# Two layers of a transformer-like block on one core: first layer and second attention in one engine block, last stores waited for by name

## What is computed

```python
x = x + tanh(g_xattn[0]) * L0_xattn(layernorm(x), ctx, ...)   # 16 heads, soft triangular mask
x = x + tanh(g_ffn[0])   * L0_ffn(layernorm(x), ...)          # 8 experts, best 2 per row, capacity per expert
x = x + tanh(g_xattn[1]) * L1_xattn(layernorm(x), ctx, ...)   # rotary positions, causal band of 128
x = x + tanh(g_ffn[1])   * L1_ffn(layernorm(x), ...)          # 16 experts, best 4 per row, and 2 shared ones
```

## Time and profile before

| what | us |
| --- | --- |
| median of 3 runs | 1760.22 |
| profiled execution, its own time | 1755.15 |
| its span, first to last instruction | 1753.3 |
| TensorE busy in it | 1574.9 (90%) |
| VectorE busy | 1237.1 (71%) |
| ScalarE busy | 1001.0 (57%) |
| GpSimd busy | 774.6 (44%) |

### The profile page before, as it was taken

The page is one execution under the profiler, slowest core; times in us unless marked ns, Lnnn a source line. Parts: engine busy times, 40 slices in busy tenths (PEclk is TensorE's granted clock), DMA queues, the critical chain, the costliest instruction groups (busy, mean ns, idle before and its releaser), DMA issues. The chain is left out here.

```text
span 1753.3 us, 45015 instructions
## 1 busy us (share of the span) xinstructions
PE 1574.9 (90%) x16664; PEld 1223.8 (70%) x16664; DVE 1237.1 (71%) x3676; ACT 1001.0 (57%) x1742; POOL 774.6 (44%) x948
## 2 busy tenths in 40 slices
PE   4799999789899999999999578898887689999997
PEld 3466666458788888888887345665554389898874
DVE  5888888856556555655577489988987366757767
ACT  5578877665345454445433355675654358677752
POOL 4356657787310000100264433332465153677765
PEclk8999999989999999999999689999999799999999
DMA  6555545243376535545462343332334456899954
GB/s 197 131 144 120 118 110 136 52 116 99 96 193 197 192 118 181 187 138 189 134 184 82 87 85 86 65 69 54 74 85 128 157 166 216 259 299 295 313 167 144
DMA packets 297740, 257.03 MB, mean 147 GB/s; under 512 B 198079, under 2 KB 270187, under 8 KB 296248
## 3 DMA queue, kind: packets, MB, share of 16 engines
q1 hardware_dynamic: 271288, 168.84, 35.7%
q0 software_dynamic: 26240, 85.32, 14.8%
HBM read 102.98 MB, written 107.74 MB: 120 GB/s over the span
## 5 line engine op out<-in xcount | busy, mean ns | idle before, releaser
L1830 PE MATMUL ps<-m_xT,m_w_halves 128*128 128x256 f16 x3360 | 413.4, 273 | 0.0
L1830 PEld LDWEIGHTS ps<-m_xT,m_w_halves 128*128 128x128 f16 x3360 | 329.1, 98 | 38.8 <-ACT a_probs L1283 0.4
L1283 ACT ACTIVATE a_probs<-ps 128x1024 f32<-128x1024 f32 (+1 forms) x256 | 234.6, 917 | 161.7 <-PE ps L1108 158.3
L1861 PE MATMUL ps<-m_w_halves,m_hiddenT 128*128 128x256 f16 x1680 | 231.2, 274 | 8.8 <-DVE m_hiddenT L1989 5.8
L1915 ACT ACTIVATE m_hiddenT<-m_hidden 128x256 f16<-128x256 f32 x280 | 116.4, 416 | 213.1 <-DVE m_hidden L1984 213.1
L1409 POOL TENSOR_TENSOR a_probs<-a_probs,a_half_above 128x512 f32<-128x512 f32 x128 | 163.8, 1282 | 127.7 <-ACT a_probs L1283 127.2
L1989 DVE TENSOR_TENSOR m_hiddenT<-m_hidden,m_hiddenT 128x256 f16<-128x256 f32 x280 | 119.1, 425 | 124.5 <-ACT m_hiddenT L1915 124.2
L1108 PE MATMUL ps<-a_Q,a_K 32*128 32x256 f16 (+1 forms) x2048 | 146.5, 262 | 65.4 <-DVE a_neg_max L1498 30.0
L1781 POOL DMA_DIRECT2D expert_out<-m_y x40 | 29.0, 725 | 382.0 <-DVE m_y L1972 189.6
L1501 DVE TENSOR_REDUCE a_qT<-ps 128x4 f16<-128x1024 f32 x128 | 156.6, 1223 | 44.4 <-PE ps L1119 43.6
L1861 PEld LDWEIGHTS ps<-m_w_halves,m_hiddenT 128*128 128x128 f16 x1680 | 163.7, 98 | 33.0 <-DVE m_hiddenT L1989 10.9
(11 more groups left out here) (312 smaller groups left out, 3015.3 us busy)
## 6 DMA issues: line engine op xcount, KB each, us to landing
routed<-m_zeros POOLq DMA_DIRECT2D x32, 768.0 KB, 4.2
r_space<-routed SPq DMA_DIRECT2D x48, 512.0 KB
routed_out<-m_y SPq DMA_DIRECT2D x48, 512.0 KB
r_w_load<-in_L_w SPq DMA_DIRECT2D x24, 896.0 KB, 7.1
dispatched<-r_x_halves SPq DMA_DIRECT2D x10, 1024.0 KB, 5.2
expert_out<-m_y POOLq DMA_DIRECT2D x40, 256.0 KB, 2.6
a_ctx_in<-in_ctx SPq DMA_DIRECT2D x32, 256.0 KB, 2.9
m_experts_load<-in_L_experts SPq DMA_DIRECT2D x18, 384.0 KB, 3.5
```

Of the source, the lines that this page charges most:

```text
L1283: A(pr[:, g % 2, 2 * jp:2 * jp + 2, :], SC[:, :, 0:SPAN], ACT.Exp, scale=1.0 / math.sqrt(DH)).then_inc(asem["ex"], 1)
L1830: last = mm(psum[:, v % HB, m * CH:(m + 1) * CH], wh[u][:, ws_, m, d_ * F0 + f_ * P:d_ * F0 + (f_ + 1) * P], xT[:, q % XB, xs_ * KT + d_, ...
L1861: last = mm(down_of(q, t), hT[:, hs_, f_, t * P:(t + 1) * P], wh[u][:, ws_, 2, f_ * D:(f_ + 1) * D], start=f_ == 0 and k == 0, stop=f_ == ...
```

## The change

The bodies of the five lists of `attention` become functions that `attention` returns (they stand one step of indentation further left and are otherwise as they were, but for the lines below). After both calls one block runs, on each engine, the first layer's list and the second attention's behind it. In place of the meeting between them SyncE, TensorE, ScalarE and GpSimd wait at the start of their second list for `m0f_y_out` at 40 (the last take), for the stores of the second layer's weights and for the zeroing; VectorE waits for the latter two only. The waits for the stores of `m_y` stand ahead of ScalarE's first exponential and of GpSimd's first gather of the second attention. The waits at the end of the first layer's lists go. In `last_rows` the take stands behind the statistics. The meeting ahead of the second layer's experts stays.

```diff
-        with nc.Block() as block:
 
-            @block.sync
-            def _(sp):
+        def sync(sp):
+            if causal_band:
+                first_layer_ended(sp)
...
-            @block.tensor
-            def _(pe):
+        def tensor(pe):
+            if causal_band:
+                first_layer_ended(pe)
...
-            @block.scalar
-            def _(act):
+        def scalar(act):
+            if causal_band:
+                first_layer_ended(act)
             A = nc.scalar.activation
 
             def exp(i, s):
                 g, jp = step(s)
                 need(act, "sc", i, s)
+                if causal_band and (i, s) == (0, 0):
+                    all_rows_stored(act)
...
-            @block.gpsimd
-            def _(pool):
+        def gpsimd(pool):
+            if causal_band:
+                first_layer_ended(pool)
...
                     newton(i, s)
+                    if causal_band and (i, s) == (min(GATHER_AT), 0):
+                        all_rows_stored(pool)
                     if causal_band and i in GATHER_AT:
...
-            @block.vector
-            def _(dve):
+        def vector(dve):
+            if causal_band:
+                first_layer_sent(dve)
...
+        return sync, tensor, scalar, gpsimd, vector
...
+    rows_stored = [sem(f"m0f_y_sent{u}") for u in range(2)]
+
+    rows_out = sem("m0f_y_out")
+    w16_sent = [sem(f"m0f_experts1_sent{u}") for u in range(2)]
+    routed_zeroed = sem("m0f_zeroed")
+    ROUTED_ZEROED = 16 * RG * (ROUTED // (P * 6))
+
+    def first_layer_sent(eng):
+        for u in range(2):
+            eng.wait_ge(w16_sent[u], 16 * 9)
+        eng.wait_ge(routed_zeroed, ROUTED_ZEROED)
+
+    def first_layer_ended(eng):
+        eng.wait_ge(rows_out, CHUNKS0)
+        first_layer_sent(eng)
+
+    def all_rows_stored(eng):
+        for u in range(2):
+            eng.wait_ge(rows_stored[u], 16 * (CHUNKS0 // 2))
...
                 store_next_layer(E1 - 1)
-                for u in range(2):
-                    sp.wait_ge(e_sent[u], 16 * (E1 // 2))
...
-                for u in range(YB):
-                    pool.wait_ge(y_sent[u], 16 * (STEPS // YB))
-                pool.wait_ge(zeroed, 16 * RG * PIECES)
...
             def last_rows(dve):
-                take(dve, STEPS - 1)
                 row_stats(dve, 1, 10)
                 mean_and_var(dve, 1, 10)
+                take(dve, STEPS - 1)
...
-    attention(0)
+    first_layer = attention(0)
     open_route1()
-    attention(1)
+    second_layer = attention(1)
+
+    with nc.Block() as block:
+
+        @block.sync
+        def _(sp):
+            first_layer[0](sp)
+            second_layer[0](sp)
...
```

More of the change, by code:

```diff
@@ new lines, in sync, with load, to_slots, slots_of_k @@
+        def sync(sp):
+            if causal_band:
+                first_layer_ended(sp)
+            def load(m):
+                need(sp, "tc", m - 2)
+                sp.dma_start(xin[:, m % 2, :, :], ctx_dram[m, :, :, :]).then_inc(ctx_in[m % 2], 16)
+            def to_slots(m, src, dst, counter):
+                need(sp, "sc", m - 4, 7)
+                need(sp, "max", m - 4, 7)
+                for t in range(TT):
+                    sp.dma_start_transpose(dst[:, m % 4, :, t * P:(t + 1) * P],
+                                           src[:, t, :, :].rearrange("p h r -> p (h r)"))\
+                      .then_inc(slots_in[counter][m % 4], 16)
+            def slots_of_k(m):
+                need(sp, "kh", m)
+                to_slots(m, kT1, K1, "k1")
+                need(sp, "kl", m)
+                to_slots(m, kT2, K2, "k2")
+            def half_of_q2(m, k):
+                if causal_band:
+                    need(sp, "neg", m, k)
+                else:
+                    need(sp, "max", m, 4 * k + 3)
+                need(sp, "qdup", m)
+                need(sp, "sc", m - 1, 4 * k + 3)
+                for t in range(TT):
+                    sp.dma_start_transpose(Q2[:, 2 * k:2 * k + 2, t * P:(t + 1) * P],
+                                           qT2[:, m % 3, t, k * 8:(k + 1) * 8, :].rearrange("p h r -> p (h r)"))\
+                      .then_inc(q2_in[k], 16)
+            load(0)
+            load(1)
+            if causal_band:
+                for k, name in (("L1_router", "router"), ("L1_e_bias", "e_bias"), ("iota", "iota"), ("less", "less"),
+                                ("tri", "tri")):
+                    whole = r1[name][:, :] if name in ("e_bias", "iota") else r1[name][:, :, :]
+                    sp.dma_start(whole, a[k]).then_inc(ld1, 16)
+                sp.wait_ge(buffers_set, 3)
+            for i in range(-3, B):
+                if 0 <= i:
+                    half_of_q2(i, 1)
+                if causal_band and 0 <= i + 2 < B:
+                    slots_of_k(i + 2)
+                if 2 <= i + 5 < B:
+                    load(i + 5)
+                if 0 <= i + 1 < B:
+                    half_of_q2(i + 1, 0)
+                if not causal_band and i == -2:
+                    sp.dma_start(x[:, 8 * TT:16 * TT, :], x_dram[:, 8 * TT:16 * TT, :]).then_inc(x_loaded[2], 16)
+                if not causal_band and 0 <= i < 10:
+                    if i == 0:
+                        sp.wait_ge(zero_set, 1)
+                    sp.dma_start(disp[i * P * 8:(i + 1) * P * 8, :].rearrange("(p t) d -> p (t d)", p=P),
+                                 r_xhl[:, 2, :, :, :].rearrange("p t s d -> p (t s d)").bitcast(F32))\
+                      .then_inc(disp_zeroed, 16)
+                if not causal_band and i == 10:
+                    for m, k in enumerate(("w1", "w3", "w2")):
+                        sp.dma_start(w_load[:, m, :], a[f"L0_{k}"][0, :, :]).then_inc(w_loaded, 16)
+                if i + 3 < B:
+                    need(sp, "qh", i + 3)
+                    need(sp, "ql", i + 3)
+                    to_slots(i + 3, qT1, Q1, "q1")
+                    if not causal_band:
+                        slots_of_k(i + 3)
+            if not causal_band:
+                first.sync(sp)
+            if causal_band:
+                sp.wait_ge(combined, 4 * B)
+                sp.dma_start(shared_weights(), w16[:, :, E1:E1 + 2, :]).then_inc(w1_in[0], 16)
+                sp.wait_ge(sent1[0], RT * 4 * 16)
+                for r in range(XB1):
+                    load_routed_rows(sp, r)
```

1163 lines of the change are left out of this document (557 added, 606 removed).

## The result

The changed kernel took 1749.36 us in the median of 4 runs (1748.31 to 1752.44), the kernel before 1759.47 in 4 runs beside them (1756.6 to 1761.05). The ratio is 0.9947, 95% interval 0.993 to 0.9964: 9.3 us less, between 6.3 and 12.3. Two later sets of runs of the same kernel gave 0.9947 (0.9928 to 0.9967) and 0.9961 (0.9947 to 0.9976). The forecast was 7.4 us less, a ratio of 0.9958, which all three intervals hold.

The account below looks back on a forecast made before the run. Bound by the meeting between layers, no engine, half its hole GpSimd's DRAIN. -8.21 + 0.25 + 0.2 + 0.4 + 0 = -7.36 us against the 1760.22 median gives 1752.9 us (chance 0.70), range 1749.5 to 1756.2.

Parts of the forecast that it names:

- The meeting, -8.21: Between first layer's last take and second attention: removing the meeting saves the whole 8.21 us hole, at least 5.3.
- the waits, +0.2: Second attention's start: seeing the take's count and passing three fulfilled waits costs 0.2 us, bounds 0.05 and 0.6.
- The take behind the statistics, +0.25: End of first layer on VectorE: statistics fill an idle gap, last copy ends 0.25 us later, bounds 0 and 1.02.
- Context load beside the store, +0.4: Second attention's opening: first context load shares transfer engines with GpSimd's last store, costing 0.4 us, bounds 0 and 0.73.
- GpSimd's memsets, 0: Second attention's opening: memsets move 6.7 us earlier, the rest 7.4; GpSimd's 4.5 us idle covers the difference, so 0.
- TensorE's clock, 0: Second attention's opening: same clock assumed for the same instructions, 0 us, between -2.5 and +1.5.
- rival 2: Opening: TensorE's shorter pause lets the clock rise sooner, 2.5 us more gain, 1750.4 us; chance 0.12.
- I let the gain pass to the end undiminished.: Behind the opening: second attention, its closing meeting and second layer's experts keep their order, so the full 7.36 us remains.
- Rival 1: Opening: waits, load, clock and take come near their bad ends, gain only about 4.5 us, 1755.7 us; chance 0.11.
- rival 3: No change that can be told: attention's end set by other work, or an engine still held; 1757 to 1760; chance 0.04.
- The slowing one: Second attention: TensorE falls to half clock in further thin stretches, about 3.1 us each; 1764 us or more; chance 0.03.
- A wait of over 2 us: Sign of being wrong: a wait over 2 us at any engine's first instruction of the second attention.

Follow-up runs that it names:

- e1: The changed kernel run again, unaltered, in five rounds; ratio to the kernel before 0.9947 (0.9928 to 0.9967).
- e2: Changed kernel with the waits for the last stores put back to the second attention's start on four engines, no meeting; one run, 1756.32 us.
- e7: Against e3: the first block ends without GpSimd's DRAIN, the meeting stays; ratio to the kernel before 0.9981 (0.9961 to 1.0).
- e3: Changed kernel with its two lists in two blocks: meeting back, no store waited for ahead of it; ratio to the kernel before 0.9997 (0.9983 to 1.0011).
- e10: The changed kernel a third time, unaltered, beside e9 on the same chip, five rounds; ratio to the kernel before 0.9961 (0.9947 to 0.9976).
- e4: Against e3: an empty block between the two, so two meetings in a row, each with its DRAIN; one run, 1764.27 us.
- e8: Changed kernel with the take ahead of the statistics and no GpSimd DRAIN at the second meeting; ratio to the kernel before 0.9963 (0.9948 to 0.9979).
- e9: e6 with no GpSimd DRAIN at the second meeting; ratio to the kernel before 0.9949 (0.9928 to 0.997).
- e6: Changed kernel with take ahead of statistics, and context loads and first normalisation ahead of the wait for the take; ratio to the kernel before 0.9966 (0.9952 to 0.9981).

## Why the prediction was right, point by point

- *The meeting, -8.21, and the waits, +0.2.* From the take's last copy to the normalisation 8.21 us became 0.04 in the first profile and in e1. The meeting's term was right whole; the waits were put too high, since the fulfilled waits behind the awaited one cost nothing that shows (0.04 us in all, under the bound of 0.05). The two parts named in the prediction were measured each by itself: the store 2.96 us (e2, 3.00 less 0.04; 2.9 by its rows), GpSimd's part of the meeting 5.38 (e7 against e3). With the 0.66 of the meeting as such they come to 9.0, not 8.17, since both of them hold GpSimd's start and its issue of the store.
- *The take behind the statistics, +0.25.* Counted from the end of the last combine, the take's end moved from 1.53 us to 1.71 (968.18 to 969.89), so +0.18. From the end of TensorE's last products it is +0.61 in the first profile, where these ended early, and +0.17 and +0.18 in e1 and e10; so the sign "under 0.5 us later" failed in the first and held in the others.
- *Context load beside the store, +0.4.* In the first profile +0.35 (transposes 3.00 us behind the issue in place of 2.65), in e1 +0.04, in e10 +0.22. In e2, e3 and e4, where the store had been issued at least 2.7 us ahead, the transposes start 2.86, 2.76 and 2.75 us behind the load's issue, so the term in the changed kernel is not told from nothing. That the transfers hold each other up shows on the store, which took 4.6 us from issue to landing in place of 2.6, off the path. The bound of +0.73 was wrong: with the store 0.32 us ahead, in e7, the term is +1.66 at the transposes, and +1.4 at the first projection. In the changed kernel SyncE's issue precedes GpSimd's by 0.27 us; that this order keeps the term small is argued from e7 alone.

Landing times of the changed kernel (KB each, median us to landing; two of the three loads start beside the store):

```profile
a_ctx_in<-in_ctx SPq DMA_DIRECT2D x3, 256.0 KB, 3.0
expert_out<-m_y POOLq DMA_DIRECT2D x1, 256.0 KB, 4.6
```

- *GpSimd's memsets, 0.* Right: GpSimd was still idle 3.67 us before its next instruction, in place of 4.5.
- *TensorE's clock, 0.* At the first projection the profiled shift is -7.39 us, at the first exponential -7.36 (38.64 against 46.00), in e10 -8.0, in e1 -8.95. The shorter pause did not bring the full clock sooner in the work: it begins 7.7 us behind the normalisation before (at 980.5), and 8.2, 8.8 and 7.4 behind it in the first profile, e1 and e10. So rival 2 did not come true. What sets e1 apart is a later stretch: the other three run at half clock for about 10 us shortly ahead of the first exponential, e1 for 3 us there and for 13 us behind it, where its attention is 2.1 us longer. So what it gained by the clock it gave back. In e1 (columns as in the earlier trace rows, clock third from the end; the first exponential starts at 1003.49):

```profile
993.40:996.40 3.00, 3.00 (x17) 1.95 (x18) 1.98 (x10) 0.00 (x0) 1.11 (x2) 0.50 0.78 176
996.80:1003.30 6.50, 3.90 (x44) 2.44 (x44) 5.64 (x28) 2.25 (x3) 2.31 (x2) 1.00 0.34 81
1003.60:1017.00 13.40, 10.96 (x89) 5.40 (x88) 9.88 (x45) 5.76 (x8) 6.37 (x6) 0.50 0.54 109
```

- *"I let the gain pass to the end undiminished."* This step failed at the second meeting, by 0.7 us. The prediction had taken that meeting to move as a whole, and had read GpSimd's DRAIN there as a price of its own. But with no DRAIN ahead of it at the first meeting any more, it grew from 5.25 to 7.23 us and came out behind VectorE. All three traces of the changed kernel show it (16.41 to 16.43 us for 15.70), and e8 and e9 take it back. That 7.2 to 8.0 us reach the end all the same is in part luck: the stretch of the second layer's experts is 0.5 to 1.0 us shorter in these three traces, which the prediction did not foresee and no run explains. So is the agreement of -7.36 to the digit at the first exponential, where the take and the waits were each off by 0.2 to 0.4.
- *Rivals.* Rival 1's 4.5 us lies outside two of the three intervals, and the traces give 7.2 to 8.0; rival 3 fell. The slowing one cost the changed kernel 2.1 us of attention in e1 and next to nothing in its two other traces. Its mechanism is there, larger, in e3 and e4, where the clock over the attention fell to 0.93 and it took 7.5 and 10.5 us longer than before, and at 5 to 6 us in e6, e7 and e9. What sets this off is open.
- *Signs of being wrong.* A wait of over 2 us at an engine's first instruction was there (ScalarE 2.99, TensorE 2.69; 10.98 and 10.15 before), but it holds the wait for the take and for the normalisation, which the change leaves in place; the bound of 2 us was too tight to tell anything.

## What to carry to other kernels

Where engines meet, read the meeting's instructions one by one: a DRAIN that moves no data can be most of it, and a wait on the one count that the next stage needs leaves it out. A DRAIN left out can be paid in part at the next one, as in the changed kernel, so look at who comes last there. Where loads on the path and a store off it start together, look at which is issued first: with the load 0.27 us ahead its wait grew by 0 to 0.35 us, with the store 0.32 us ahead, in one trace, by 1.66.

## What was not expected of the hardware

GpSimd's DRAIN is no fixed price: 46 ns right behind another DRAIN (e4), 4.57 us behind the first layer's block, 5.25 behind the second attention with a DRAIN at its front and 7.23 without one, the last the same to within 0.01 us in five kernels. A store still on its way does not make it longer (e3). Nor does a DRAIN that is left out always come back: in e8, where the second meeting has none, the one at the end of the kernel takes no longer than in the changed kernel, where it has one (ns, the changed kernel first; 12.6 us in e9 and 12.7 before the change).

```profile
L2174 POOLq DRAIN  x1: 12814/12814/12814, 1730.9 to 1730.9; - x1
...
L2174 POOLq DRAIN  x1: 12709/12709/12709, 1728.5 to 1728.5; - x1
```

What of GpSimd's work sets the length these runs do not tell. And a store and two context loads of 256 KB each, the first load issued 0.32 us behind the store on another queue, took 4.4 and (median of the two) 4.3 us to land (e7), where the store without the loads took 2.6 and the loads without the store 2.7 to 3.0 (before, e2, e3, e4): more than the 0.73 us that the rates of the earlier trace rows would add.
